# A style-conditioned convolution stack in front of a mixture of experts: layer 0 on four-position blocks with two terms for three, and layer 1's input in planes put together by 4 copies for 16

## The chip, the cores and the metric

The kernel runs on one core of a Trainium2 chip. The metric is the device time of one execution in microseconds; less is better. TensorE (PE) does the matmuls, VectorE (DVE), ScalarE (ACT) and GpSimd (POOL) the elementwise work, and SyncE (SP) issues most DMAs. Each engine runs its own instruction stream in program order and waits on semaphores.

## What is computed

The input is 128 samples of 32 channels and 512 positions. Four convolution layers with kernels that depend on the sample's style (`same`, `upsample`, `same`, `downsample`) turn x into hidden states of the same shape. Each of the 128 x 32 = 4096 rows of 512 is then a token for a layer of 16 experts with top-4 routing and one shared expert; the sum is added to x. Cut to what matters:

```python
def _layer(x, style, w, b, mw, mb, typ):
    s = style @ mw.T + mb                       # one factor for each sample and input channel
    weight = SCALE * w * s[:, None, :, None]
    demod = lax.rsqrt(jnp.sum(weight * weight, axis=(2, 3)) + EPS)
    weight = weight * demod[:, :, None, None]
    # 'same': 3-tap convolution; 'upsample': transposed convolution, then blur;
    # 'downsample': blur, then 3-tap convolution of stride 2
...
scores = sigmoid(x @ gate_w.T) + bias
topk_w, topk_idx = jax.lax.top_k(scores, 4)
...
out = sum over the experts of cw * (silu(x @ Wg.T) * (x @ Wu.T)) @ Wd.T
out = out + silu(x @ Sg.T) * (x @ Su.T) @ Sd.T
return x_input + out
```

## The kernel before

Every product is made at nearly full float32 precision from float32r halves: each operand is split into a high part and a low part (the rest), and a product is three matmuls, high x high, high x low and low x high. `hi_passes` (L202) issues the two that need only the high part of the data, `lo_passes` (L209) the third, which also needs the low part. So a convolution of n terms (n matrices against n shifted views of the data) is 3n matmuls.

**Groups.** The convolution stage works through G = 32 groups of 4 samples x 32 channels = 128 partitions. `body(g)` is written for each engine, and the engines' bodies are one software pipeline: in body g PE does layer 0 of group g + 1, layers 1, 2 and 3 of group g, and for group g - 1 the transposes, the shared expert's products and the router's logits. Its order is: layer 0, prefix of the masks, transposes, layer 1, up products, layer 2, turning z, logits, down products, layer 3. The order is written out by hand, and only semaphores tie the engines together. Most bodies run in a loop of two bodies a turn.

**Layout.** In layers 1 to 3 a matrix of 128x128 holds the taps for four positions at once: partitions are 4 positions (Q = 4) x 32 channels, and the free dimension is sample and block. Layer 0 is different: partitions are 4 samples x 32 channels, a matrix is block diagonal over the samples, and the three taps are three matrices against x0 shifted by 0, 1 and 2 positions. As each partition has its own sample and channel, its style factor is one scalar (`own`, filled by `owns` in the start), applied by ACT in `first_in` (L497, x0_hi) and by DVE in `first_in` (L716, x0_lo), both reading `xraw`.

**From layer 0 to layer 1.** ACT evacuates bank 0 into t1 with one instruction (L511), even and odd positions apart. DVE splits t1 into x1p (high L766, low L760). SP's `stack` (L300) then copies x1p to x1, in which the partitions are 4 shifted positions x 32 channels: 16 copies from SBUF to SBUF, one for each of 4 position planes and 4 samples, of 32 partitions x 2 x 255 or 256 elements. Layer 1 on PE waits for `x1_stacked`, and so does DVE before it writes x1p again.

**The chain on DVE.** DVE's body g does the placement of group g - 2 (L777 to L786), xt_lo (L790), x1p of group g + 1, x2 of group g in two halves (L800, L802, L760), the gated product z (L808, L809), x3 of group g in two halves (L826, L831, L760), the router's top-4 for group g - 1 (L839 to L859), then x0_lo of group g + 2 (L716) and the output row (L867). PE's low passes of layer 0 wait for x0_lo.

**GpSimd** fills constants in the start, waits for `fill_written` (three DMAs of SP behind its loads), issues two DMAs, and in the stage issues four indirect DMAs a group, the `scatter` of the group's list entries, when DVE's placement is ready. **SP** issues, in each body: the stack of group g + 1, the load of xraw for group g + 3, the output and the next xbase, and four writes of h_rows.

After the stage follow the tables of the expert jobs and the expert stage (from about 600 us), which the change doesn't touch.

## Time and profile before

| | |
|---|---|
| median of 3 runs | 1265.27 us (1263.3 to 1267.74) |
| the profiled execution | 1267.31 us, its span 1265.6 us |
| PE, DVE, ACT, GpSimd busy | 91%, 68%, 38%, 43% of the span |
| start, 0 to 60 us | PE busy 31.85 us |
| groups, 60 to 560 us | PE busy 465.04 us, DVE 402.86 us, ACT 248.40 us, GpSimd 126.03 us |
| between the stages, 560 to 600 us | PE busy 14.38 us |
| experts, from 600 us | PE busy 645.70 us |
| mean granted TensorE clock | 0.97 of full speed |

The profile is of one execution, on its one core. Busy times count instructions that run; an idle time stands in brackets ahead of the instruction that ends it, with the instruction that released it. A matmul's length includes its filling; the distance from one start to the next says how fast they follow each other.

### The profile page before, as it was taken

The numbers are of one execution on the slowest core, as the hardware profiler recorded it, in microseconds if no ns is written. First come the engines' busy times: TensorE is split into PE (matmuls) and PEld (weight loads), VectorE is DVE, ScalarE is ACT, GpSimd is POOL, SyncE is SP. The second block draws the span as 40 slices with busy tenths as digits, with TensorE's granted clock in tenths as the row PEclk, the third lists the DMA queues.
The fourth block names the chain that finished last, engine by engine and source line by source line (L and its number), as shares of the span: only waits on it lengthen the run. The fifth ranks groups of instructions, "written<-read, shape, count | busy, mean of one in ns | idle before, by whom it ended". The sixth has DMA issues, their size and how long they took to land. (4 is left out here: it accounts for less than half of the span.)

```text
span 1265.6 us, 25736 instructions
## 1 busy us (share of the span) xinstructions
PE 1157.0 (91%) x7065; PEld 996.7 (79%) x7066; DVE 857.2 (68%) x2456; ACT 483.0 (38%) x1087; POOL 545.5 (43%) x634
## 2 busy tenths in 40 slices
PE   4699999999999999982999999999999999999995
PEld 3476777777777777761998999999998988999995
DVE  8387788878887878875556565655656665555653
ACT  4354445545544454431333232332324332232321
POOL 0012222222222222232565656666666565666663
PEclk9699999999999999995999999999999999999998
DMA  4356444444444444432666766576666767666664
GB/s 153 89 132 179 121 126 129 126 128 129 129 127 128 129 128 131 119 82 92 147 120 151 127 152 120 112 160 120 152 119 159 193 113 162 116 115 116 109 113 77
DMA packets 115059, 162.24 MB, mean 128 GB/s; under 512 B 22880, under 2 KB 72096, under 8 KB 113504
## 3 DMA queue, kind: packets, MB, share of 16 engines
q0 software_dynamic: 35616, 74.08, 32.0%
q1 hardware_dynamic: 78128, 87.93, 24.6%
q10 hardware_dynamic: 1296, 0.01, 0.1%
q8 instruction: 7, 0.11, 0.0%
q14 instruction: 12, 0.10, 0.0%
HBM read 73.28 MB, written 55.18 MB: 102 GB/s over the span
## 5 line engine op out<-in xcount | busy, mean ns | idle before, releaser
L388 POOL DMA_INDIRECT lists<-entry,place x128 | 134.2, 1048 | 431.2 <-DVE place L786 400.0
L1178 PE MATMUL bank<-xt_hi,wup_hi 128*128 128x256 f32 x1104 | 271.8, 281 | 1.9 <-ACT xt_hi L594 1.6
L1178 PE MATMUL bank<-xt_hi,wup_lo 128*128 128x256 f32 x1104 | 271.9, 280 | 0.0
L419 POOL DMA_INDIRECT out_rows<-yb,sid x140 | 228.1, 1629 | 89.8 <-DVE yb L959 64.8
L1178 PEld LDWEIGHTS bank<-xt_hi,wup_hi 128*128 128x128 f32 x1104 | 208.9, 189 | 6.8 <-ACT xt_hi L594 2.0
L1178 PEld LDWEIGHTS bank<-xt_hi,wup_lo 128*128 128x128 f32 x1104 | 207.9, 188 | 2.8
L406 POOL DMA_INDIRECT xg<-h_rows,gid x140 | 141.4, 1010 | 112.7 <-PE bank L1156 65.8
L1182 PE MATMUL bank<-xt_lo,wup_hi 128*128 128x256 f32 x1104 | 173.8, 280 | 0.0
L959 DVE TENSOR_SCALAR yb<-bank,all_lists 128x512 f32<-128x512 f32 x138 | 100.3, 748 | 90.8 <-DMA out_rows<-yb,sid 57.0
L202 PE MATMUL bank<-x_hi,cwt_hi 128*128 128x512 f32 (+1 forms) x352 | 139.8, 400 | 13.9 <-DVE x_hi L831 10.5
L502 ACT ACTIVATE t<-bank,cB,cA 128x256 f32<-128x256 f32 x256 | 127.3, 569 | 59.8 <-PE bank L209 50.4
L1182 PEld LDWEIGHTS bank<-xt_lo,wup_hi 128*128 128x128 f32 x1104 | 148.8, 188 | 0.0
L611 ACT ACTIVATE zt_hi<-z 128x256 fp32r<-128x256 f32 x138 | 57.6, 418 | 229.1 <-DVE z L949 219.1
L202 PE MATMUL bank<-x_hi,cwt_lo 128*128 128x512 f32 (+1 forms) x352 | 138.0, 392 | 0.0
L607 ACT ACTIVATE sg<-bank 128x256 f32<-128x256 f32 x138 | 52.7, 382 | 209.7 <-PE bank L1182 184.6
L209 PE MATMUL bank<-x_lo,cwt_hi 128*128 128x512 f32 (+1 forms) x352 | 105.2, 400 | 21.5 <-DVE x_lo L716 21.5
L1194 PE MATMUL bank<-wdn_hi,zt_hi 128*128 128x512 f32 x276 | 115.1, 417 | 2.4 <-ACT zt_hi L611 2.4
L1196 PE MATMUL bank<-wdn_hi,zt_lo 128*128 128x512 f32 x276 | 109.2, 396 | 0.0
L1194 PE MATMUL bank<-wdn_lo,zt_hi 128*128 128x512 f32 x276 | 108.9, 395 | 0.0
L202 PEld LDWEIGHTS bank<-x_hi,cwt_hi 128*128 128x128 f32 x352 | 67.9, 193 | 42.0 <-issue 23.7
L209 PEld LDWEIGHTS bank<-x_lo,cwt_hi 128*128 128x128 f32 x352 | 63.3, 194 | 47.8 <-DVE x_lo L716 34.9
L760 DVE TENSOR_TENSOR zt_lo<-z,zt_hi 128x256 fp32r<-128x256 f32 x138 | 58.8, 426 | 61.9 <-ACT zt_hi L611 54.7
(208 smaller groups left out, 2105.7 us busy)
## 6 DMA issues: line engine op xcount, KB each, us to landing
x<-x1p SPq DMA_DIRECT2D x256, 64.0 KB
x<-x1p SPq DMA_DIRECT2D x256, 63.8 KB
wraw<-in_Wup SPq DMA_DIRECT2D x11, 1024.0 KB
xraw<-in_x SPq DMA_DIRECT2D x32, 256.0 KB, 2.6
xbase<-in_x SPq DMA_DIRECT2D x32, 256.0 KB
h_rows<-hrow SPq DMA_DIRECT2D x128, 64.0 KB
out_rows<-orow SPq DMA_DIRECT2D x32, 256.0 KB, 2.0
wdraw<-in_Wdn SPq DMA_DIRECT2D x11, 512.0 KB
```

What stands on the lines that cost most here:

```text
L202: r = pe.matmul(dst, lhs[a if data_moves else 0], rhs[0 if data_moves else a], start=n == 0 and a == 0, stop=False)
L209: r = pe.matmul(dst, lhs[0 if data_moves else 1], rhs[1 if data_moves else 0], start=False, stop=last and n == len(terms) - 1)
L388: pool.indirect_dma_start(out=lists, out_offset=bass.IndirectOffsetOnAxis(ap=place[:, par, k:k + 1], axis=0), in_=entry[:, par, k, :], in_ ...
L406: pool.indirect_dma_start(out=xg[:, u, :], out_offset=None, in_=h_rows, in_offset=bass.IndirectOffsetOnAxis(ap=gid[:, u:u + 1], axis=0)).t ...
L419: pool.indirect_dma_start(out=out, out_offset=bass.IndirectOffsetOnAxis(ap=sid[:, u:u + 1], axis=0), in_=yb[:, u, :], in_offset=None, comp ...
L502: r = act.activation(dst[:, n], src[:, n], ACT.Identity, scale=cA[:, l, bass.ds(g * NB + b, 1)], bias=cB[:, l, bass.ds(g * NB + b, 1)])
L760: return dve.tensor_tensor(lo, src, hi.bitcast(F32), ALU.subtract)
L959: dve.tensor_scalar(yb[:, u, :], bank[6 + u][:], all_lists[:, bass.ds(at + u, 1), 1], None, ALU.mult).then_inc(S["b_y"], 1)
L1178: pe.matmul(dst, lhs[a], rhs[0], start=k == 0 and a == 0, stop=False)
L1182: r = pe.matmul(dst, lhs[0], rhs[1], start=False, stop=k == HC - 1)
L1194: pe.matmul(bank[6 + u][:], zt[0][:, u, c, :], wdn[b][a][:, c, :], start=c == 0 and a == 0, stop=False)
L1196: r = pe.matmul(bank[6 + u][:], zt[1][:, u, c, :], wdn[b][0][:, c, :], start=False, stop=c == IC - 1)
```

## The change

The host lays x out a second time, as `xq`: partitions are 4 positions x 32 channels, with 4 samples x 130 blocks, one position of padding ahead of the row (and zeros behind). Layer 0 then has the layout of the later layers: each matrix holds the taps for four positions, and two matrices (this block and the next) take the place of three. Its output has 4 positions in the partitions and 4 samples x 128 blocks in the free dimension.

- One partition now carries all four samples, so that the style factor is no longer a scalar of the partition. `own` and `owns` fall away. GpSimd multiplies `xraw` in place by `s` (`scaled`, new), ACT only copies to x0_hi and waits for GpSimd (`xs_ready`), DVE subtracts to get x0_lo. Four `scaled` stand ahead of GpSimd's loop, the others in it, each ahead of the scatter of four groups before.
- ACT's evacuation of layer 0 is four instructions by `evac`, one for each sample, where it was one.
- x1p is 4 positions x 32 channels by now, so x1 is made from it by 4 copies of 96 or 32 partitions. x1, t2, x2 and t3 keep even and odd blocks in two planes of 128. In layer 2 the second matrix needs the next block, which lies in the other plane; its matmuls are made for each plane, 256 columns each.
- xraw, x0_hi and x0_lo have 520 columns, where they had 512, 514 and 514.

The core of the diff (the changed memsets, shapes and waits of the same kind are left out):

```diff
-    UP, SAME, DOWN, SQ = K, K + 1, K + 3, K + 6
+    FIRST, UP, SAME, DOWN, SQ = 0, 2, 3, 5, 8
...
+    V = L // Q
+    VP = xq.shape[3]
+    STACKS = 4
...
-        xraw = sb("xraw", [P, 2, L])
+        xraw = sb("xraw", [P, 2, NB, VP])
-        x0 = [sb("x0_hi", [P, L + 2], F32R), sb("x0_lo", [P, L + 2], F32R)]
-        x1p = sb("x1p", [P, 2, 2, L // 2], F32R)
-        x1 = sb("x1", [P, 2, NB, W], F32R)
-        x2 = [sb("x2_hi", [P, NB, W + 2], F32R), sb("x2_lo", [P, NB, W + 2], F32R)]
+        x0 = [sb("x0_hi", [P, NB, VP], F32R), sb("x0_lo", [P, NB, VP], F32R)]
+        x1p = sb("x1p", [P, 2, NB, V], F32R)
+        x1 = sb("x1", [P, 2, NB, 2, V], F32R)
+        x2 = [sb("x2_hi", [P, NB, 2, V + 2], F32R), sb("x2_lo", [P, NB, 2, V + 2], F32R)]
...
 # SP, stack(g)
-                for q, (plane, src, dst) in enumerate(((1, 0, 1), (0, 0, 0), (1, 0, 0), (0, 1, 0))):
-                    n = W - src - dst
-                    for b in range(NB):
-                        sp.dma_start(x1[C * q:C * q + C, :, b, dst:dst + n].bitcast(F32),
-                                     x1p[C * b:C * b + C, :, plane, src:src + n].bitcast(F32)).then_inc(S["x1_stacked"], 16)
+                for plane, to, part, rows, back in ((0, 1, 0, 3, 0), (0, 0, 3, 1, 1), (1, 0, 1, 3, 0), (1, 3, 0, 1, -1)):
+                    dst = slice(max(back, 0), V + min(back, 0))
+                    src = slice(max(-back, 0), V + min(-back, 0))
+                    sp.dma_start(x1[C * to:C * (to + rows), :, :, plane, dst].rearrange("p a b u -> p (a b) u").bitcast(F32),
+                                 x1p[C * part:C * (part + rows), :, :, src].rearrange("p a b u -> p (a b) u").bitcast(F32)).then_inc(S["x1_stacked"], 16)
...
 # GpSimd
-            with pool.Fori(0, G // 2) as it:
+            def scaled(g, par, k):
+                pool.wait_ge(S[f"x_loaded{par}"], 16 * (k + 1))
+                land(pool)
+                pool.tensor_tensor(xraw[:, par], xraw[:, par], s[:, 0, bass.ds(g * NB, NB)].rearrange("p (b a) -> p b a", a=1).broadcast_to([P, NB, VP]),
+                                   ALU.mult).then_inc(S["xs_ready"], 1)
+
+            pool.wait_ge(S["s_ready"], 1)
+            for g in range(4):
+                scaled(g, g % 2, g // 2)
+            with pool.Fori(0, (G - 4) // 2) as it:
                 for u in range(2):
+                    scaled(it * 2 + (u + 4), u, it + 2)
                     scatter(it * 2 + u, u)
+            for g in range(G - 4, G):
+                scatter(g, g % 2)
...
 # ACT, first_in and layer0
-                act.wait_ge(S[f"x_loaded{par}"], 16 * (k + 1))
+                act.wait_ge(S["xs_ready"], g + 1)
                 land(act)
-                act.activation(x0[0][:, 1:L + 1], xraw[:, par, :], ACT.Copy, scale=own[:, 0, bass.ds(g, 1)]).then_inc(S["x0_hi"], 1)
+                act.activation(x0[0][:], xraw[:, par], ACT.Copy).then_inc(S["x0_hi"], 1)
...
-                act.activation(t1[:], bank[0][:].rearrange("p (w two) -> p two w", two=2), ACT.Identity,
-                               scale=own[:, 1, bass.ds(g, 1)], bias=own[:, 2, bass.ds(g, 1)]).then_inc(S["t1_ready"], 1)
+                evac(g, range(NB), bank[0][:].rearrange("p (b v) -> p b v", b=NB), t1, 0, S["t1_ready"])
...
 # DVE, first_in
-                dve.scalar_tensor_tensor(out=x0[1][:, 1:L + 1], in0=xraw[:, par, :], scalar=own[:, 0, bass.ds(g, 1)],
-                                         in1=x0[0][:, 1:L + 1].bitcast(F32), op0=ALU.mult, op1=ALU.subtract).then_inc(S["x0_lo"], 1)
+                minus(x0[1][:], xraw[:, par], x0[0][:]).then_inc(S["x0_lo"], 1)
...
 # PE, layer0
-                same = [([w[:, k, :] for w in cwt], [x[:, k:k + L] for x in x0], True) for k in range(K)]
+                dst = bank[0][:].rearrange("p (b v) -> p b v", b=NB)
+                same = [columns(FIRST + m, P, lambda a: x0[a][:, :, m:m + V]) for m in range(2)]
...
 # PE, layer 2
-                        terms = [columns(SAME, P, lambda a: x2[a][:, both, 0:W]),
-                                 columns(SAME + 1, P, lambda a: x2[a][:, both, 1:W + 1])]
+                        here = [columns(SAME, P, lambda a: x2[a][:, both, :, 0:V])]
+                        following = [[columns(SAME + 1, P, lambda a: x2[a][:, both, 1 - r, r:r + V])] for r in range(2)]
...
-                        hi_passes(pe, dst, terms)
+                        hi_passes(pe, dst, here)
+                        for r in range(2):
+                            for a in range(2):
+                                pe.matmul(dst[:, :, r], cwt[a][:, SAME + 1, :], following[r][0][1][0], start=False, stop=False)
...
-                        lo_passes(pe, dst, terms).then_inc(S["l2_done"], 1)
+                        lo_passes(pe, dst, here, last=False)
+                        for r in range(2):
+                            ins = lo_passes(pe, dst[:, :, r], following[r], last=r == 1)
+                        ins.then_inc(S["l2_done"], 1)
```

How the instructions stand on GpSimd, from the two DMAs of the start to the loop of the stage. Before, with `lists<-entry,place` the scatter and L392 the loop:

```order
L382 DMA out_rows<-zrow 128x512 x2
L392 UNCONDITIONAL_BRANCH
L392 ISA
L388 DMA lists<-entry,place 65536x2 x4
L385 REGISTER_ALU
L388 DMA lists<-entry,place 65536x2 x4
L392 REGISTER_ALU
L392 COMPARE_AND_BRANCH
```

Now, with `xraw<-xraw,s` the new product:

```order
L386 DMA out_rows<-zrow 128x512 x2
L399 TENSOR_TENSOR xraw<-xraw,s 128x520 x4
L405 UNCONDITIONAL_BRANCH
L405 ISA
L399 ISA
L399 TENSOR_TENSOR xraw<-xraw,s 128x520
L389 REGISTER_ALU
L392 DMA lists<-entry,place 65536x2 x4
L399 ISA
L399 TENSOR_TENSOR xraw<-xraw,s 128x520
L389 REGISTER_ALU
L392 DMA lists<-entry,place 65536x2 x4
```

Each scatter of the loop has a product ahead of it, and four products stand between the start's DMAs and the loop.

On PE, layer 0 in body 2, ahead of the prefix of the masks (`bank<-mask,tri`). Before:

```order
L202 MATMUL bank<-x_hi,cwt_hi 128x512
L202 MATMUL bank<-x_hi,cwt_lo 128x512
L202 MATMUL bank<-x_hi,cwt_hi 128x512
L202 MATMUL bank<-x_hi,cwt_lo 128x512
L202 MATMUL bank<-x_hi,cwt_hi 128x512
L202 MATMUL bank<-x_hi,cwt_lo 128x512
L209 MATMUL bank<-x_lo,cwt_hi 128x512 x3
L1043 MATMUL bank<-mask,tri 128x16
```

Now:

```order
L206 MATMUL bank<-x_hi,cwt_hi 128x512
L206 MATMUL bank<-x_hi,cwt_lo 128x512
L206 MATMUL bank<-x_hi,cwt_hi 128x512
L206 MATMUL bank<-x_hi,cwt_lo 128x512
L213 MATMUL bank<-x_lo,cwt_hi 128x512 x2
L1048 MATMUL bank<-mask,tri 128x16
```

Two high passes and one low pass are gone.

On SP, the first stack, with the load of xraw behind it; `h_rows<-zrow` and `lists<-all_lists` are the fills that GpSimd waits for. Before:

```order
L290 DMA h_rows<-zrow 128x512 x2
L291 DMA lists<-all_lists 128x1024
L300 DMA x<-x1p 32x2x255 x4
L300 DMA x<-x1p 32x2x256 x8
L300 DMA x<-x1p 32x2x255 x4
L306 DMA xraw<-in_x 128x512
```

Now:

```order
L293 DMA h_rows<-zrow 128x512 x2
L294 DMA lists<-all_lists 128x1024
L304 DMA x<-x1p 96x8x128
L304 DMA x<-x1p 32x8x127
L304 DMA x<-x1p 96x8x128
L304 DMA x<-x1p 32x8x127
L310 DMA xraw<-in_xq 128x520
```

Sixteen copies of 32 partitions have become two of 96 and two of 32, and the load of xraw stands twelve copies nearer.

## Rows read from the trace of the kernel before

**Rows 1.** The stretch of the 32 groups: busy time (and instructions) of each engine.
```profile
60.00:560.00 500.00, 465.04 (x2223) 359.13 (x2221) 402.86 (x1488) 248.40 (x549) 126.03 (x120) 1.00 0.49 128
```

**Rows 2.** Page, part 2: granted clock of TensorE, 40 slices of 31.6 us.
```profile
PEclk9699999999999999995999999999999999999998
```

**Rows 3.** Waits from 60 to 560 us: total us, times, longest.
```profile
PE bank L209 <- DVE x_lo L716: 20.4, 29, 1.0
```

**Rows 4.** Timeline of PE: the first and the last of those 29 waits.
```profile
72.47 0.96 PE L209 MATMUL bank<-x_lo,cwt_hi 128*128 128x512 f32 x3 [0.52 <-DVE x_lo L716]
...
533.84 0.97 PE L209 MATMUL bank<-x_lo,cwt_hi 128*128 128x512 f32 x3 [0.52 <-DVE x_lo L716]
```

**Rows 5.** Timeline of PE in one group: start, length, idle before.
```profile
303.13 0.97 PE L209 MATMUL bank<-x_lo,cwt_hi 128*128 128x512 f32 x3 [0.78 <-DVE x_lo L716]
...
307.74 1.09 PE L209 MATMUL bank<-wup_hi,xt_lo 128*128 128x512 f32 x4
...
315.44 0.48 PE L202 MATMUL bank<-x_hi,cwt_hi 128*128 128x512 f32 x1 [0.58 <-DVE x_hi L831]
```

**Rows 6.** Timeline of ACT in the same group.
```profile
305.17 0.78 ACT L511 ACTIVATE t<-bank,own 128x512 f32<-128x512 f32 x1
...
311.39 1.02 ACT L502 ACTIVATE t<-bank,cB,cA 128x256 f32<-128x256 f32 x2 [2.14 <-PE bank L209]
...
318.15 1.50 ACT L502 ACTIVATE hrow<-bank,cB,cA 128x128 f32<-128x128 f32 x4 [1.28 <-PE bank L209]
```

**Rows 7.** Timeline of DVE in the same group.
```profile
312.47 0.06 DVE L826 MEMSET t<- 64x2 f32 x1 [1.40 <-issue]
...
313.03 0.69 DVE L760 TENSOR_TENSOR x_lo<-t,x_hi 128x512 fp32r<-128x512 f32 x1
...
319.09 0.75 DVE L716 SCALAR_TENSOR_TENSOR x_lo<-xraw,own,x_hi 128x512 fp32r<-128x512 f32 x1
```

**Rows 8.** GpSimd in the same group: the last of the four scatter issues.
```profile
310.71 0.97 POOL L388 DMA_INDIRECT lists<-entry,place  x1 [0.30 <-issue]
```

**Rows 9.** Timeline of PE in the expert stage.
```profile
800.24 0.28 PE L1178 MATMUL bank<-xt_hi,wup_hi 128*128 128x256 f32 x1
800.36 0.28 PE L1178 MATMUL bank<-xt_hi,wup_lo 128*128 128x256 f32 x1
```

**Rows 10.** SP's queue in the same group.
```profile
307.48 10.20 SPq L300 DMA_DIRECT2D x<-x1p  x16
```

**Rows 11.** Packets of one queue, 28 to 40 us, then 57 to 60.5 us.
```profile
q1 hardware_dynamic: 1296, 1.08, 38.2%
...
q1 hardware_dynamic: 576, 0.26, 29.6%
```

**Rows 12.** Timeline of the start, all engines.
```profile
16.00 0.71 ACT L497 ACTIVATE x_hi<-xraw,own 128x512 fp32r<-128x512 f32 x1
...
18.60 1.38 POOL L382 DMA_DIRECT2D out_rows<-zrow  x2 [16.09 <-DMA lists<-all_lists]
...
19.70 1.75 DVE L723 RECIPROCAL d<-dv 128x256 f32<-128x256 f32 x1 [0.64 <-ACT dv L568]
...
22.02 0.76 DVE L671 COPY own<-cA 32x32 f32<-32x32 f32 x4
...
26.95 0.42 DVE L766 CAST x1p<-t 128x512 fp32r<-128x512 f32 x1
...
28.13 10.35 SPq L300 DMA_DIRECT2D x<-x1p  x16
...
40.08 0.77 PE L202 MATMUL bank<-x,cwt_hi 128*128 128x512 f32 x1 [9.61 <-DMA x<-x1p]
```

**Rows 13.** GpSimd operations that read, and DVE beside the second.
```profile
1.96 0.29 POOL L373 TENSOR_SCALAR_AFFINE_SELECT ident<-ident 128x128 f32<-128x128 f32 x1 [0.16 <-POOL ones L371]
...
958.95 0.72 POOL L429 COPY sid<-sid_next 128x2 int32<-128x2 int32 x1
958.96 1.28 DVE L749 TENSOR_TENSOR wup_lo<-wraw,wup_hi 128x512 fp32r<-128x512 f32 x2
```

More of the change, by code:

```diff
@@ L248, in matrices @@
                 rows = slice(C * q, C * q + C)
-                copy(big[rows, 0:K, q, :], mats[rows, 0:K])
                 copy(big[rows, SQ:SQ + 4, q, :], mats[rows, NT:NT + 4])
@@ L665, in _ @@
             dve.memset(tsum[:], 0.0).then_inc(S["consts_done"], 1)
-            def owns(n, a):
-                for b in range(NB):
-                    rows = slice(C * b, C * b + C)
-                    r = dve.tensor_copy(own[rows, n, :], a[rows, 0, :].rearrange("p (g b) -> p g b", b=NB)[:, :, b])
-                return r
             dve.wait_ge(S["taps_loaded"], 16 * Q)
@@ L1014, in turn_z, with columns @@
                 return r
+            def columns(m, rows, data):
+                return [w[0:rows, m, :] for w in cwt], [data(a) for a in range(2)], True
             def layer0(g):
@@ L1020, in layer0 @@
                     pe.wait_ge(S["t1_ready"], g)
[L1021 removed]
+                dst = bank[0][:].rearrange("p (b v) -> p b v", b=NB)
+                same = [columns(FIRST + m, P, lambda a: x0[a][:, :, m:m + V]) for m in range(2)]
                 pe.wait_ge(S["x0_hi"], g + 1)
[L1023 removed]
+                hi_passes(pe, dst, same)
                 pe.wait_ge(S["x0_lo"], g + 1)
[L1025 to L1029 removed]
+                lo_passes(pe, dst, same).then_inc(S["l0_done"], 1)
             def body(g, par, tail=0):
```

67 lines of the change are left out of this document (33 added, 34 removed).

## Prediction

> **What bounds the kernel now.** I read the stages first. Between 60 and 560 us, where the 32 groups run, PE is busy 465 of 500 us at full granted clock, DVE 403, ACT 248, GpSimd 126 [rows 1, 2]. So the change touches a stage in which PE nearly always works, and the first thought is that each matmul removed is time won. The waits correct this: PE stands 29 times, 0.70 us on average, in front of the same instruction, the first low pass of layer 0, until DVE has written x0_lo [rows 3]. The first and the last of these waits end at 72.47 and 533.84 us [rows 4], so 28 groups take 16.48 us each.
>
> In one group at 303 us, PE starts the low passes of layer 0 at 303.13 after a wait of 0.78; the other wait of note is for DVE's x3_hi at 315.44, 0.58 [rows 5]. The loop closes through three engines: PE (from the layer-0 low passes to the first half of layer 2) -> ACT (evacuates that half at 311.39 [rows 6]) -> DVE (starts on it at 312.47 and works almost without a gap through x3, the logits and the top-4 to x0_lo at 319.09 [rows 7]) -> PE. What PE does between layer 2 and the layer-0 high passes is not on this loop. So the group is timed by PE's first half and DVE's second half, and a saving or a delay counts only if it lies on that loop.
>
> **Layer 0, nine matmuls to six.** A full 512-column matmul follows the last one after (1.09 - 0.40)/3 = 0.23 us [rows 5]. Four of the six passes that are kept stand ahead of the x0_lo wait, as six of nine did: the two removed there only lengthen the wait. One low pass is removed behind it: -0.23 us a group on the loop. x0_lo itself becomes a plain subtraction: 0.75 [rows 7] to what L760 takes for 512 columns, 0.69, and 1.6% for 520: -0.05. Sum -0.28; 28 groups: -8 us. If PE alone set the pace, it would be 3 x 0.23 x 28 = -19 us; that is the far bound on the good side.
>
> **Layer 2, split into halves.** Per group, six 512-column matmuls become twelve of 256 columns. In the expert stage 256-column matmuls, each with its own weight load, follow each other at 0.12 us [rows 9], half of 0.23: nothing gained or lost.
>
> **ACT's evacuation of layer 0** goes from one instruction of 0.78 to four of 128 columns. Four such take 1.50 us for hrow [rows 6]: +0.72 us. ACT is busy half of the stage [rows 1], but behind this instruction it evacuates layer 1, and DVE waits for both: x1p and then x2 come later. What hides it is that DVE reaches t1 only after its eight placement operations, and that PE has the expert's up products between layer 1 and layer 2. I cost it at nothing; with that cover gone it is at most 0.72 a group, 20 us.
>
> **The stack of x1, 16 copies to 4.** SP issues 16 in 10.2 us [rows 10]. The bytes stay; packets go from 1024 or 1020 bytes to 512 or 508, so there are 2048 for 1024. A packet of the present stack takes 0.382 x 16 x 12 us / 1040 = 70 ns, counting the sixteen semaphore writes of each copy as free; a 512-byte packet of h_rows 0.296 x 16 x 3.5 / 512 = 32 ns [rows 11]. The new stack therefore occupies the 16 engines for 4.1 us at 32 ns up to 9.0 us at 70 ns. I take 5.5. In the loop that hides: the issue ends at 317.7 [rows 10], and PE takes the stack in layer 1 of the next group, behind the layer-0 wait, at about 321; the new one is through earlier. Only the first stack, at 28 us, is waited for: 9.61 us of PE [rows 12].
>
> **GpSimd multiplies xraw by the style.** This is new: 32 products of 128x520 with two SBUF inputs, in place, one for each group, put ahead of each group's scatter. The trace has no such operation. From below: no faster than DVE's 0.69 for a product-like operation of 512 columns [rows 7]. From above: an affine_select reads and writes 128 columns in 0.29 us [rows 13]; four times that is 1.18, and doubled for the second input 2.4. I take 1.2, since the 0.29 holds a fixed part. GpSimd has the time (126 us of 500), and ACT needs the result a group later.
>
> The question is DVE. A GpSimd copy of two elements took 0.72 us, against 0.29 for 128 columns, when it began at 958.95 beside DVE's subtraction of two SBUF tensors at 958.96, and ended when the first of the two was over [rows 13]. So the two engines exclude each other there. The reverse, DVE behind a long GpSimd read, no row shows: its price lies between 0 and the whole operation. The Trainium skill (SBUF — State Buffer, "Who interferes with whom") says that whoever issues first holds the shared pair for the whole instruction and the other "fully blocks". It thus speaks against this change: by that rule DVE loses most of the product's length in each group, case (c) below; of it this trace shows the one order, DVE first and GpSimd waiting, and the other not. The Trainium skill (GPSIMD Engine Reference, "Elementwise — side-by-side cycle accounting") has 4497 ns for 2048 columns of such a sum, by which an estimate for 520 is 1.14 us, and the term below would be +26 us.
>
> Where does it fall? SP starts the stack at about 307.5 and has issued its four copies after 2.6 us at today's 0.65 each [rows 10]; xraw follows and queues behind the stack's data. With 1.6 us of latency (40.08 less the end of issue, 38.48 [rows 12]) and 4.1 to 9.0 us of data it lands between 313 and 318 us of this group. GpSimd's scatter is over at 311.7 [rows 8]. So the product starts inside DVE's run from 312.47 to 319.84, which is on the loop, and not in the idle 1.40 us before it [rows 7]. Almost all of DVE there is of the excluded kind: casts and subtractions from SBUF, then small operations that wait for each other. If DVE waits for the product, it loses about 1.0 of the 1.2 us (some reads of PSUM go on). I take 1.0 us for 27 groups: +27 us. What is behind DVE's waiting instruction is x3, then the whole top-4 chain and x0_lo; PE would wait longer at both places.
>
> **The start.** Today ACT makes x0_hi at 16.00. GpSimd, which must now come first, stands until 18.60 for the fill of the lists and then issues two DMAs for 1.38 us [rows 12]; 1.2 of product follow: 21.2. ACT's x0_hi ends at 21.9 instead of 16.7. Behind it on ACT stand the table load and the square root: DVE's reciprocal, now at 19.70, starts about 23.9, +4.2. DVE's copies into own fall away (0.76 for cA, the like for cB): -1.5. So x1p moves from 26.95 by +2.7. From the first stack issue at 28.13 to PE at 40.08 were 11.95 us [rows 12]; with 5.5 us of data, and 2.5 for the first packet's and the last landing's latency, about 8: -4. Start together: -1.3, between -3 (data 4.1) and +2.5 (data 9.0). One further group with layer 0 at the end of its chain gives -0.7.
>
> **Sum.** -8 - 1.3 - 0.7 + 27 = +17 us on the profiled execution's 1267.3 (span 1265.6 and 1.7 around it), which is 2.0 above the median of the runs: 1265.3 + 17 = 1282 us.
>
> **Rivals.**
>
> (a) GpSimd's product costs DVE nothing: it waits or reads between DVE's operations, as the short copy did without delaying the next DVE instruction. Then -10: 1255 us, faster. For it speaks that DVE's pair in [rows 13] took 1.28 us, twice 0.69 less the usual overlap: the copy did not hold up the second. The sign turns at a delay of 10/27 = 0.37 us a group. Chance 0.34.
>
> (b) It costs a part, 0.25 to 0.5 us a group, since it begins late in DVE's run or gets in only at a gap: 1262 to 1269 us. Chance 0.12.
>
> (c) My forecast, 0.6 to 1.2 us a group: 1271 to 1288. Chance 0.42.
>
> (d) The waits grow so long that the granted clock falls. It fell only in the slices of the start and of the end of the stage, 0.6 and 0.5 on the page [rows 2], where PE idled for microseconds. A twentieth of the stage at half clock would add 25 us: 1300 or more. Chance 0.07.
>
> (e) Issue of the large copies grows with their packets: 10.2 us for 1024 packets would be 20 us for 2048, more than a group of 16.5. SP would then set the pace, +4 us a group, 1390 us. All 16 copies today are issued at the same cadence with data hardly filling the engines (38%), so I give it 0.05.
>
> **How the numbers follow.** What a measurement of this kernel tells from no change is about 0.3%, 4 us. Faster: (a), less where the ACT term eats into it, and nothing of the rest: 0.35. Within: most of (b): 0.10. Slower: (c), (d), (e) and the rest of (b): 0.55. The range must take in (a) and (c) and leaves out the ends of (d) and (e) and the best of (a): 1251 to 1292. Case (c) alone would be 1271 to 1288.
>
> **What would show it.** In the profile after: 256-column matmuls of layer 2 at 0.12 us; a layer-0 wait of about 0.70 + 0.47 us on x0_lo; the product's length, and where it lies; DVE's subtractions of 0.69 and its casts that are stretched or late beside it, and a group above 17 us where (c) holds, 16.2 where (a) does; PE's first layer-1 matmul at about 39 us. I am wrong if DVE's durations stay what they were with the product beside them, or if the copy lands late.

## The result and the profile after

The changed kernel takes 1293.82 us (median of 4 runs, 1288.15 to 1298.19), the kernel before 1264.7 us in its runs (1263.3 to 1267.74): ratio 1.0225, 95% interval 1.0199 to 1.025. The forecast was 1282 us in a range of 1251 to 1292.

The page and the stretch from 60 to 560 us of the changed kernel (busy time, PE's row of tenths, granted clock; then one row of the windows view, its columns as in [rows 1]):

```profile
PE 1157.5 (89%) x7160; PEld 996.7 (77%) x7161; DVE 868.6 (67%) x2444; ACT 499.3 (39%) x1185; POOL 581.6 (45%) x666
...
PE   3798888888889898894699999999999999999995
...
PEclk9799999999999999997799999999999999999998
```
```profile
60.00:560.00 500.00, 436.03 (x2187) 333.76 (x2186) 394.49 (x1409) 247.39 (x602) 151.19 (x140) 0.99 0.45 123
```

PE's tenths fall from 9 to 8 in most slices of the loop, while its granted clock stays as in [rows 2]: PE waits more, it doesn't run slower. Its waits in the same stretch (total us, times, longest), beside the 20.4 us of [rows 3]:

```profile
PE bank L213 <- DVE x_lo L721: 32.2, 27, 1.5
PE bank L206 <- DVE x_hi L835: 20.3, 26, 1.5
PE bank L206 <- ACT zt_hi L558: 7.4, 10, 1.0
```

The timeline of the changed kernel, from the start to the last group used below (start, duration, in brackets the idle time before and what ended it):

```profile
21.15 2.10 POOL L399 TENSOR_TENSOR xraw<-xraw,s 128x520 f32<-128x520 f32 x2
...
31.77 2.87 SPq L304 DMA_DIRECT2D x<-x1p  x4
38.31 0.77 PE L206 MATMUL bank<-x,cwt_hi 128*128 128x512 f32 x1 [4.67 <-DMA x<-x1p]
71.27 0.19 PE L1048 MATMUL bank<-mask,tri 128*128 128x16 bf16 x1
268.13 0.39 ACT L554 ACTIVATE sg<-bank 128x256 f32<-128x256 f32 x1
269.42 0.17 PE L206 MATMUL bank<-x_hi,cwt_hi 128*128 128x4 f32 x1
271.88 1.02 ACT L518 ACTIVATE t<-bank,cB,cA 128x256 f32<-128x256 f32 x2 [3.36 <-PE bank L213]
272.95 0.06 DVE L830 MEMSET t<- 64x2 f32 x1 [2.19 <-ACT t L518]
312.06 1.05 POOL L399 TENSOR_TENSOR xraw<-xraw,s 128x520 f32<-128x520 f32 x1 [3.74 <-DMA xraw<-in_xq]
312.13 1.00 DVE L721 TENSOR_TENSOR x_lo<-t3f,x_hi 64x4 fp32r<-64x4 f32 x1
329.45 0.70 DVE L721 TENSOR_TENSOR x_lo<-t,x_hi 128x512 fp32r<-128x512 f32 x1
329.49 1.57 POOL L399 TENSOR_TENSOR xraw<-xraw,s 128x520 f32<-128x520 f32 x1 [3.78 <-DMA xraw<-in_xq]
330.85 0.24 DVE L846 TENSOR_TENSOR sc<-sig,biasrow 128x16 f32<-128x16 f32 x1 [0.28 <-ACT sig L570]
559.68 0.19 PE L1048 MATMUL bank<-mask,tri 128*128 128x16 bf16 x1
```

The reader is to see four things.
- **Start.** The first two products take GpSimd 2.10 us from 21.15 on. The four copies are issued in 2.87 us for the 10.35 of [rows 12], and layer 1 begins at 38.31 for 40.08.
- **Loop.** The matmul of mask and tri stands once in each group. From its first to its 29th there are 488.41 us, 17.44 us a group; before it is 461.37 and 16.48. The whole stage, from the first to the 32nd of them, takes 531.3 us for 503.6: this is the loss.
- **The product and DVE keep each other out.** At 312.13 a DVE operation on 64x4 elements takes 1.00 us and ends with GpSimd's product of 1.05; the same operation takes 0.17 where GpSimd is idle. In the next group DVE's subtraction of 0.70 at 329.45 was there first and GpSimd takes 1.57. In 18 of the first 28 groups an operation of DVE is 0.5 to 0.9 us longer for it; these groups take 18.1 us on average, the others 16.2. Over the 28 groups DVE's operations beside the product are 13.8 us longer in all, 0.49 a group.
- **Layer 2's evacuation starts late.** The first half of layer 2 ends on PE where the 128x4 matmul of the second half starts (269.42). ScalarE, idle since 268.52, starts to evacuate it only at 271.88, and DVE waits 2.19 us for that. I call the distance from that 128x4 matmul to the evacuation the **lag**. Over the 28 groups it has a mean of 1.61 us and is mostly near 0.4, 1.0, 1.7 or 2.5. Before, its mean is 0.72 and its highest value 1.35. The prediction doesn't speak of it. The trace's semaphore records, which no view prints, tell more: the signal by which PE says that the first half is done comes at 271.64, 2.22 us behind the start of the 128x4 matmul, and ScalarE's wait ends 0.02 us later. The signal is recorded in 25 of the 32 groups, and in all of these the wait ends within 0.03 us of it. Where the lag is 0.4 us (after_2 below) the signal comes 0.18 us behind the 128x4 matmul. So ScalarE isn't slow to answer: PE's completion of the half, or its signal, is late. The ends of matmuls are modelled in the profile, so that the trace can't say which of the two.

The expert stage, which the change doesn't touch, adds its own: from the first transpose of gathered rows to the end 676.1 us for 670.8.

### The profile page after: what moved, and what is told of

The parts are those of the page before. It is cut to its first block and busy times, and to the rows that moved or that the text cites. A ratio compares the mean times of both kernels' runs of the same rounds, so it can differ in the third digit from the quotient of the medians.

```text
span 1296.5 us, 25739 instructions
## 1 busy us (share of the span) xinstructions
PE 1157.5 (89%) x7160; PEld 996.7 (77%) x7161; DVE 868.6 (67%) x2444; ACT 499.3 (39%) x1185; POOL 581.6 (45%) x666
## 3 DMA queue, kind: packets, MB, share of 16 engines
q0 software_dynamic: 35616, 74.08, 32.2%
## 5 line engine op out<-in xcount | busy, mean ns | idle before, releaser
L1190 PE MATMUL bank<-xt_hi,wup_hi 128*128 128x256 f32 x1104 | 275.3, 282 | 1.8 <-ACT xt_hi L609 1.5
L1190 PE MATMUL bank<-xt_hi,wup_lo 128*128 128x256 f32 x1104 | 274.8, 282 | 0.0
L392 POOL DMA_INDIRECT lists<-entry,place x128 | 133.9, 1046 | 266.6 <-DVE place L789 235.4
L518 ACT ACTIVATE t<-bank,cB,cA 128x256 f32<-128x256 f32 (+1 forms) x384 | 172.1, 541 | 86.8 <-PE bank L213 65.8
L206 PE MATMUL bank<-x_hi,cwt_hi 128*128 128x512 f32 (+1 forms) x256 | 105.9, 417 | 32.1 <-DVE x_hi L835 22.9
L213 PE MATMUL bank<-x_lo,cwt_hi 128*128 128x512 f32 (+2 forms) x384 | 99.9, 368 | 33.0 <-DVE x_lo L721 33.0
L399 POOL TENSOR_TENSOR xraw<-xraw,s 128x520 f32<-128x520 f32 x32 | 38.0, 1189 | 151.5 <-DMA xraw<-in_xq 151.5
L206 PE MATMUL bank<-x_hi,cwt_lo 128*128 128x512 f32 (+1 forms) x256 | 100.9, 394 | 0.0
```

Of the source, the lines that this page charges most:

```text
L206: r = pe.matmul(dst, lhs[a if data_moves else 0], rhs[0 if data_moves else a], start=n == 0 and a == 0, stop=False)
L213: r = pe.matmul(dst, lhs[0 if data_moves else 1], rhs[1 if data_moves else 0], start=False, stop=last and n == len(terms) - 1)
L392: pool.indirect_dma_start(out=lists, out_offset=bass.IndirectOffsetOnAxis(ap=place[:, par, k:k + 1], axis=0), in_=entry[:, par, k, :], in_ ...
L518: r = act.activation(dst[:, n], src[:, n], ACT.Identity, scale=cA[:, l, bass.ds(g * NB + b, 1)], bias=cB[:, l, bass.ds(g * NB + b, 1)])
L1190: pe.matmul(dst, lhs[a], rhs[0], start=k == 0 and a == 0, stop=False)
```

## The experiments

Behind the first measurement the runs fall into five groups, each on one chip and each with the kernel before timed beside it. That showed two kinds of chip: **slow chips**, where it takes 1265 to 1268 us (the first measurement was on one), and **fast chips**, where it takes 1251. There were three measurements on each kind. The five groups were on five different chips (that of the first measurement isn't on record), so it isn't shown that the chip makes the difference, and not, say, something that changed between the groups; "fast chip" stands for "the chips on which the kernel before took 1251 us". So a kernel's loop is compared only with loops on the same kind. Even there it differs: the changed kernel's group is 17.44 us on one slow chip and 17.29 on another, 15.93 and 15.95 on two fast chips; so a difference between two slow chips is good to some 0.15 us. The group and the lag of a row come from one profiled execution each. "Group" is the distance from the first to the 29th matmul of mask and tri, divided by 28; where an edit changes numbers, tokens go to other experts and the expert stage changes its length (a_noprod adds 142 blocks of rows to the output, the kernel before 140), so only the group is compared there, and the ratio beside "output differs" says little.

| kernel | chip | first, 29th, us | group, us | mean lag, us | ratio to before (95%) |
|---|---|---|---|---|---|
| before | slow | 73.27, 534.64 | 16.48 | 0.72 | 1 |
| changed | slow | 71.27, 559.68 | 17.44 | 1.61 | 1.0225 (1.0199–1.025) |
| after_4 (changed) | slow | 70.89, 555.12 | 17.29 | 1.36 | 1.0215 (1.018–1.0251) |
| b_two | slow | 72.54, 526.02 | 16.20 | 0.59 | 0.9937 (0.9913–0.9962), output differs |
| b_evac4 | slow | 72.33, 543.91 | 16.84 | 1.03 | 1.0088 (1.0054–1.0121) |
| a_onevac_2 | slow | 70.29, 527.46 | 16.33 | 0.77 | 0.9981 (0.9956–1.0005), output differs |
| a_noprod_onevac | slow | 67.69, 516.66 | 16.03 | 0.83 | 1.0148 (1.0109–1.0187), output differs |
| a_split4_unroll | slow | 71.53, 542.00 | 16.80 | 1.19 | 1.014 (1.0111–1.017) |
| before_2 (before) | fast | 73.26, 519.66 | 15.94 | 0.41 | 1 |
| after_2, after_3 (changed) | fast | 71.46, 517.52 and 70.31, 516.80 | 15.93, 15.95 | 0.41 | 1.0023 (1.0006–1.0041), 1.0011 (0.9992–1.0029) |
| a_noprod | fast | 68.48, 507.38 | 15.67 | 0.41 | 1.0048 (1.0034–1.0062), output differs |
| a_onevac | fast | 69.73, 510.18 | 15.73 | 0.41 | 0.9991 (0.9975–1.0008), output differs |
| a_unroll, a_unroll_2 | fast | 69.93, 518.49 and 70.93, 516.34 | 16.02, 15.91 | 0.31 | 1.0009 (0.9991–1.0028), 1.0018 (1.0–1.0037) |
| a_stack16 | fast | 73.30, 520.12 | 15.96 | 0.41 | 1.0065 (1.0045–1.0085) |
| b_product | fast | 76.86, 531.63 | 16.24 | 0.41 | 1.0103 (1.0071–1.0134) |
| b_unroll | fast | 71.74, 516.95 | 15.90 | 0.32 | 1.0001 (0.9981–1.0021) |
| a_scale4 | fast | 66.81, 524.35 | 16.34 | 0.45 | 1.0096 (1.0062–1.013) |
| a_split4 | fast | 68.85, 511.41 | 15.81 | 0.41 | 0.999 (0.9972–1.0008) |

**a_noprod** leaves the product out.

```diff
-                pool.tensor_tensor(xraw[:, par], xraw[:, par], s[...], ALU.mult).then_inc(S["xs_ready"], 1)
+                pool.sem_inc(S["xs_ready"], 1)
```


> The changed kernel with the product of x and s left out (GpSimd only passes the semaphore on, so layer 0 reads x without s). If the collision of GpSimd's product with DVE carries the loss, the loop falls from 531.3 us to about 496 (503.6 less 8) and the time to about 1257 us. If ScalarE's late start of layer 2's evacuation carries it (1.5 us behind its matmuls on average after, 0.75 before), that lag stays and only the stretched DVE operations go, 0.7 to 0.9 us in about 17 groups: about 1280 us.

**a_onevac** puts one activation in the place of the four that evacuate layer 0.

```diff
-                evac(g, range(NB), bank[0][:].rearrange("p (b v) -> p b v", b=NB), t1, 0, S["t1_ready"])
+                act.activation(t1[:]..., bank[0][:], ACT.Identity, scale=cA[:, 0, bass.ds(g * NB, 1)],
+                               bias=cB[:, 0, bass.ds(g * NB, 1)]).then_inc(S["t1_ready"], 1)
```


> The changed kernel with layer 0's result evacuated by one activation of 128x512 with one sample's scale, in place of four of 128x128 (the numbers of three samples in four are scaled wrongly). If ScalarE's four evacuations make it late, ScalarE gains 0.6 to 0.8 us a group, the lag in layer 2 falls back to 0.4 to 1.3 us and the time to 1265 to 1275 us. If the product alone carries the loss: 1288 to 1294 us.

**a_unroll** writes ScalarE's loop out (b_unroll is the same in the kernel before).

```diff
-            with act.Fori(0, (G - 6) // 2) as it:
-                body(it * 2 + 3, 1, (it + 1, it + 2))
-                body(it * 2 + 4, 0, (it + 2, it + 2))
+            for g in range(3, G - 3):
+                body(g, g % 2, (g // 2, (g + 1) // 2))
```


> The changed kernel with ScalarE's loop over groups 3 to 28 written out, so that its scales' places are constants and no register is worked out ahead of an activation; nothing else differs. If ScalarE's lag comes from its instruction stream (register instructions and waits on registers), it falls to 0.3 us as in the written-out group at 71.3 us and the time to about 1270 us or less. If it comes from DMA traffic or the product, nothing changes: 1288 to 1298 us.

**a_stack16** splits each of the four stack copies by sample.

```diff
-    STACKS = 4
+    STACKS = 16
...
+                    for b in range(NB):
+                        sp.dma_start(x1[C * to:C * (to + rows), :, b, plane, dst]..., x1p[C * part:C * (part + rows), :, b, src]...)
```


> The changed kernel with each of the four stack copies split by sample, 16 copies again. If the bulk of four copies in 2.8 us delays ScalarE, its lag falls back to 0.4 to 1.3 us and the time by some 15 us, to about 1278; x_raw also lands some 7 us later, so the product falls elsewhere in the group. If the four copies have no part in it: the issue of 10 us stays hidden and the time is 1288 to 1298 us, unless the later product hits another DVE operation.

All four ran on one fast chip and were within 1% of the kernel before, where 1.02 was the base of every expectation. a_noprod's 1257.78 us is the time expected of a collision that carries the loss, but its loop stage took 480.2 us where 496 was expected. The group was short in a_noprod (15.67 us) and in a_onevac (15.73), and in a_stack16 and a_unroll, which keep product and evacuations, as well (15.96, 16.02). The long lags were gone in all four. No one edit can have done that, and the changed kernel itself hadn't run on that chip, so both kernels ran again.

**before_2 and after_2**, unchanged.

> The kernel before once more, on the chip of the runs beside it. If the chip matters, ScalarE's lag in layer 2 is a steady 0.4 us here as in the last four runs, a group takes under 16.3 us and the time is 1250 to 1255 us. If those runs owed it to their edits, the lag is 0.4 to 1.3 us as in the trace of before, a group 16.48 us.

> The changed kernel once more. If its lag of 1.0 to 2.6 us is the change's own, it is here too and the ratio to before is about 1.02 (1.020 to 1.025 measured first). If it belongs to the chip of the first run, the lag is 0.4 us, groups take about 15.9 us and the ratio is about 1.00.

Timelines of before_2, then of after_2:

```profile
73.26 0.18 PE L1043 MATMUL bank<-mask,tri 128*128 128x16 bf16 x1
519.66 0.18 PE L1043 MATMUL bank<-mask,tri 128*128 128x16 bf16 x1
1139.06 0.38 PE L1156 MATMUL bank<-ident,xg 128*128 128x128 f32 x2
1176.15 0.38 PE L1156 MATMUL bank<-ident,xg 128*128 128x128 f32 x2
```
```profile
71.46 0.18 PE L1048 MATMUL bank<-mask,tri 128*128 128x16 bf16 x1
253.19 0.17 PE L206 MATMUL bank<-x_hi,cwt_hi 128*128 128x4 f32 x1
253.61 1.02 ACT L518 ACTIVATE t<-bank,cB,cA 128x256 f32<-128x256 f32 x2 [1.33 <-PE bank L213]
258.67 1.05 POOL L399 TENSOR_TENSOR xraw<-xraw,s 128x520 f32<-128x520 f32 x1 [4.08 <-DMA xraw<-in_xq]
259.13 0.62 DVE L846 TENSOR_TENSOR sc<-sig,biasrow 128x16 f32<-128x16 f32 x1 [0.28 <-ACT sig L570]
517.52 0.19 PE L1048 MATMUL bank<-mask,tri 128*128 128x16 bf16 x1
1133.95 0.27 PE L1168 MATMUL bank<-ident,xg 128*128 128x128 f32 x1
1171.41 0.27 PE L1168 MATMUL bank<-ident,xg 128*128 128x128 f32 x1
```

Here ScalarE's evacuation follows 0.41 to 0.42 us behind the 128x4 matmul in every looped group of both kernels, and the loop is worth nothing either way (15.94 and 15.93). The product now meets the tail of DVE's operation on `sc` (0.62 us, 0.17 alone; on average 0.24 us over in the looped groups). So the loss of 27.7 us in the loop is not the change's on every chip: it appears on the slow chips. On a fast chip the parts can be read one by one. The product costs 15.93 − 15.67 = 0.26 us a group, the four evacuations 15.93 − 15.73 = 0.20, and the rest of the change gives 15.94 − (15.73 − 0.26) = 0.47 back. Sixteen copies for four change nothing in the loop (15.96), but the first group comes at 73.30 for 71.46.

**b_product** adds to the kernel before only the product, in place on `xraw` with the factors of `own`.

```diff
+                pool.tensor_tensor(xraw[:, par, :], xraw[:, par, :], own[:, 0, bass.ds(g, 1)].broadcast_to([P, L]), ALU.mult)...
...
-                act.activation(x0[0][:, 1:L + 1], xraw[:, par, :], ACT.Copy, scale=own[:, 0, bass.ds(g, 1)])
+                act.activation(x0[0][:, 1:L + 1], xraw[:, par, :], ACT.Copy)
```


> The kernel before with one thing of the change: the product of x and s on GpSimd in place in x_raw (128x512), ScalarE's copy and DVE's subtraction without a scale. If the product's collision with DVE costs 0.7 to 0.9 us in a group, 1.015 of before; if it falls where DVE has nothing due, 1.000.

> The kernel before with ScalarE's loop over groups 3 to 28 written out. If register work and waits on registers hold ScalarE up by 0.4 us a group on average (lag 0.72 to 0.31), 0.990 of before on a chip where the lag is 0.72; if the lag is a steady 0.4, 0.996 to 1.000.

The product costs 0.30 us a group here and 3.6 us at the start: 76.86 for 73.26. In the changed kernel it is 3.0 us at the start (71.46 for a_noprod's 68.48). b_unroll takes 0.1 us off the lag and nothing measurable off the time: where the signal comes in time, ScalarE's register work costs nothing.

**a_scale4** has no product; ScalarE and DVE scale by sample. **a_split4** cuts the product into four instructions. after_3 is the changed kernel.

```diff
a_scale4
-                act.activation(x0[0][:], xraw[:, par], ACT.Copy).then_inc(S["x0_hi"], 1)
+                for b in range(NB):
+                    r = act.activation(x0[0][:, b], xraw[:, par, b], ACT.Copy, scale=s[:, 0, bass.ds(g * NB + b, 1)])
...
+                    r = dve.scalar_tensor_tensor(out=x0[1][:, b], in0=xraw[:, par, b], scalar=s[:, 0, bass.ds(g * NB + b, 1)],
+                                                 in1=x0[0][:, b].bitcast(F32), op0=ALU.mult, op1=ALU.subtract)
a_split4
+                for b in range(NB):
+                    r = pool.tensor_tensor(xraw[:, par, b], xraw[:, par, b], s[:, 0, bass.ds(g * NB + b, 1)].broadcast_to([P, VP]), ALU.mult)
```


> The changed kernel a third time, to see which kind of chip this call has: with ScalarE's lag a steady 0.4 us, groups of 15.9 us and a ratio of 1.00, as in after_2, or with a lag of 1.0 to 2.6 us, groups of 17.4 us and 1.02, as in the first measurement. It is the base for the runs beside it.

> The changed kernel without the product: ScalarE writes x0_hi by four activations with the sample's scale, DVE x0_lo by four scalar_tensor_tensor, GpSimd only scatters. If the product costs 0.26 us a group and 3 us at the start, and the longer ScalarE and DVE work is hidden, the time is 10 us under the changed kernel (0.994 of before). If four short instructions for one cost their 0.7 us on ScalarE and 0.3 us on DVE as the evacuation's did (0.20 us a group in all), 1.000 to 1.003.

> The changed kernel with GpSimd's product in four instructions of 128x130. If one GpSimd instruction keeps DVE out until it ends, DVE waits at most for a quarter, 0.3 us, and its excess on the instruction that meets the product falls from a mean of 0.24 us to 0.1 or less: 2 to 4 us less than the changed kernel. If four starts on GpSimd lengthen the whole, DVE meets more pieces and the time is the same or up to 5 us more.

> The changed kernel with ScalarE's loop written out, once more. On a chip where the changed kernel's lag is 0.4 us: 0.31 us, and within 0.3% of the changed kernel, as in a_unroll. On a chip where it is 1.0 to 2.6 us: if ScalarE's looping instruction stream is what makes it late, 0.3 us here too, and 1.5 to 2% less than the changed kernel; if not, no difference.

Two rows of a_scale4's timeline, and one of a_split4's:

```profile
203.20 1.31 ACT L508 ACTIVATE x_hi<-xraw,s 128x130 fp32r<-128x130 f32 x4
...
213.23 1.15 DVE L722 SCALAR_TENSOR_TENSOR x_lo<-xraw,s,x_hi 128x130 fp32r<-128x130 f32 x4
```
```profile
207.73 1.48 POOL L400 TENSOR_TENSOR xraw<-xraw,s 128x130 f32<-128x130 f32 x4 [3.98 <-DMA xraw<-in_xq]
```

Without the product and with one instruction each, the group took 15.67 us; with four short ones for one on both engines, 16.34. That is 0.67 us a group, more than twice the product that it saves. Four pieces of product take GpSimd 1.48 us for 1.05, and yet the group is 0.14 us shorter than after_3's, as expected if DVE waits for a piece and not for the whole. With 1243.0 us its profiled span is the shortest of all, but its ratio of 0.999 can't be told from 1. a_unroll_2 repeats a_unroll: nothing gained.

**A slow chip** came next. after_4 is the changed kernel, a_split4_unroll has the product in four instructions and ScalarE's loop written out. b_two leaves the third tap out of layer 0's sum in the kernel before; b_evac4 evacuates layer 0 there with four instructions.

```diff
b_two
-                same = [([w[:, k, :] for w in cwt], [x[:, k:k + L] for x in x0], True) for k in range(K)]
+                same = [... for k in range(2)]
b_evac4
+                for n in range(4):
+                    r = act.activation(t1[:, :, 64 * n:64 * n + 64], bank[0][:, 128 * n:128 * n + 128]..., ACT.Identity, ...)
```


> The changed kernel a fourth time, as the base of this call: lag 0.4 us, 15.9 us a group and a ratio of 1.000 to 1.003, or, on a chip like that of the first measurement, a lag of 1.0 to 2.6 us and 1.02.

> The changed kernel with the product in four instructions and ScalarE's loop written out: the version that the runs so far point to. If both gains hold, 15.75 us a group and a ratio of 0.998; on a chip with the lag of the first measurement it tells whether a written-out stream ends the lag: then 0.31 us and a ratio of 0.98 to 0.99, else 1.01 or more.

> The kernel before with layer 0 in two terms for three (taps 0 and 1; the third is left out of the sum), nothing else. If only one low pass of layer 0 lies on the loop, as the prediction has it: 0.25 to 0.30 us a group less than the kernel before, 15.65 on a chip with 15.94. If all three passes do: 0.7 us less, 15.25. If the loop is DVE's at that place: nothing. The output differs, and with it which experts the tokens go to, so the loop is compared and not the end.

> The kernel before with layer 0's result evacuated by four activations of 128x128 in place of one of 128x512, with the same scale. If the four lie on the loop, as the difference between the changed kernel and a_onevac says, 0.20 us a group more (16.14 on a chip with 15.94), a ratio of 1.004; if they are covered, as the prediction has it, no difference.

A group of a_split4_unroll, then one of b_evac4 and its first and 29th groups:

```profile
243.41 0.17 PE L206 MATMUL bank<-x_hi,cwt_hi 128*128 128x4 f32 x1
245.76 1.02 ACT L519 ACTIVATE t<-bank,cB,cA 128x256 f32<-128x256 f32 x2 [3.32 <-PE bank L213]
```
```profile
72.33 0.18 PE L1045 MATMUL bank<-mask,tri 128*128 128x16 bf16 x1
...
227.85 0.41 ACT L541 ACTIVATE sg<-bank 128x256 f32<-128x256 f32 x1
229.13 0.18 PE L202 MATMUL bank<-x_hi,cwt_hi 128*128 128x4 f32 x1
231.57 1.02 ACT L502 ACTIVATE t<-bank,cB,cA 128x256 f32<-128x256 f32 x2 [3.31 <-PE bank L209]
...
543.91 0.18 PE L1045 MATMUL bank<-mask,tri 128*128 128x16 bf16 x1
```

The loss is back with the chip. A written-out stream does not end the lag (2.35 us in the group shown), so the theory that register work on ScalarE makes it falls. b_evac4 shows lags of up to 2.5 us in the old kernel, with no product, no new stack copies and no new layer 0: four evacuations are enough to lengthen it from a mean of 0.72 to 1.03. They cost 0.36 us a group, 0.9% in all. b_two gives 0.28 us a group. Both are set against the 16.48 of another slow chip; b_evac4's ratio, measured beside the kernel before on its own chip, agrees (11 us, of which 28 groups at 0.36 are 10). On the same chip as after_4, a_split4_unroll's group is 0.49 us shorter, with a mean lag of 1.19 for 1.36: on a slow chip the product in one piece costs more than the 0.14 us of a fast one.

**The last two**, on a slow chip again, undo the evacuations with and without the product (edits as above).

> The changed kernel with layer 0 evacuated in one activation, product kept. On a chip with before at 1251 us: 15.7 us a group, as in a_onevac. On a chip with before at 1265 us: if the evacuations carry most of the loss there, the lag is back at 0.4 to 0.8 us and the ratio at 1.000 to 1.005; if the product does, 1.01 or more.

> The changed kernel without the product of x and s and with layer 0 evacuated in one activation with one sample's scale. If the two costs add up on a chip with before at 1251 us: 15.94 less 0.26 less 0.20, about 15.5 us a group; if they overlap, 15.65. On a chip with before at 1265 us: a lag of at most 0.72 us and about 15.9 us a group. The output differs, so the loop is compared.

```profile
70.29 0.19 PE L1049 MATMUL bank<-mask,tri 128*128 128x16 bf16 x1
294.49 1.05 POOL L399 TENSOR_TENSOR xraw<-xraw,s 128x520 f32<-128x520 f32 x1 [3.49 <-DMA xraw<-in_xq]
294.54 1.55 DVE L722 TENSOR_TENSOR x_lo<-t,x_hi 128x512 fp32r<-128x512 f32 x1
359.44 0.69 DVE L722 TENSOR_TENSOR x_lo<-t,x_hi 128x512 fp32r<-128x512 f32 x1
359.56 1.48 POOL L399 TENSOR_TENSOR xraw<-xraw,s 128x520 f32<-128x520 f32 x1 [3.67 <-DMA xraw<-in_xq]
527.46 0.19 PE L1049 MATMUL bank<-mask,tri 128*128 128x16 bf16 x1
```

These are rows of a_onevac_2. On a slow chip one activation for four takes the changed kernel from 17.29 or 17.44 to 16.33 us a group, below the 16.48 of before. That is 0.96 to 1.11 us for 28 groups, 27 to 31 us, about all that was lost. The product then costs 16.33 − 16.03 = 0.30, much as on a fast chip. The rows show how: of the groups with a lag near 1.0 us, eight have the product begin just ahead of DVE's subtraction, which grows from 0.69 to 1.55 us, and take 16.9 to 17.0 us; in five the subtraction is first, GpSimd waits, and they take 16.1 to 16.2. So a collision in which DVE loses costs about its length, as the prediction has it; it happens in some groups only.

One run is missing: the changed kernel without the product but with its four evacuations, on a slow chip. So the 0.96 to 1.11 us is what the evacuations cost beside the product. In the old kernel, without it, they cost 0.36. The 0.60 to 0.75 us between, 17 to 21 us in 28 groups, is there only with both, and taking the product away might have undone it too.

## Why the prediction was wrong

On the first chip the sign was right and the time was 12 us short of the measured one; the reason given for the loss was one part of it. The sign was luck in so far as the chip decided it: on fast chips the same change makes no difference of note (1.0023 and 1.0011). Between the two profiled executions lie +31 us where the sum has +17: −2.0 before the first group, +27.7 in the loop stage, for which the sum has −8 and +27, and +5.3 in the expert stage, for which it has nothing. Point by point:

- **Layer 0, one low pass on the loop, −0.28 us a group: right.** b_two, which has the fewer passes and not the plain subtraction, measures 0.28, its slightly lower mean lag included, for the 0.23 of the pass. PE's waits for x0_lo grew from 0.70 to 1.19 us on average (32.2 us in 27 waits), in after_2 to 1.17 (33.9 in 29); 1.17 was forecast. The whole of the change without product and evacuations gives 0.45 to 0.47 back; the 0.17 to 0.19 above the third term come from parts that I costed at nothing and didn't try apart.
- **ScalarE's evacuation, +0.72 us, costed at nothing: this is the step that failed.** The prediction named 20 us as its price if the cover is gone, and took no case for it. It costs 0.20 us a group (5.6 us) on a fast chip; on a slow one 0.36 us without the product (b_evac4) and 0.96 to 1.11 us a group, 27 to 31 us, beside it (a_onevac_2). There it lengthens the lag behind layer 2. The trace of before had that lag already (0.31 to 1.35 us), and I read none of it: I asked whether ScalarE was busy, and it was idle for long stretches; I didn't ask how late the signal that it waited for came.
- **GpSimd's product, 1.0 us of DVE for 27 groups: the mechanism was right, the size not.** DVE and GpSimd do exclude each other, and the product takes 1.05 us where 1.2 was estimated. But on a fast chip it meets the tail of one short operation. Undone, it gives 0.26 to 0.30 us a group, 7 to 8 us for 27. The 0.5 to 0.9 us in 18 groups of the first measurement, 13.8 us in all, came with the lag: with few exceptions (two in after_4), the product falls on a long piece of layer 2's part only where DVE starts late on it. In a_split4_unroll, groups with a lag of 1.6 us take 17.2 us; in the changed kernel, with the product in one piece and a lag of 1.7 us, 17.75. So DVE's own loss beside the product is half of the sum's 27 us, and that only on the slow chips; what else the loop lost goes with the lag, which the sum doesn't have. How much of that lag needs the product too is open, as said above.
- **Start, −1.3 us: nearly right, by two errors that cancel.** It was −1.8 for layer 1 and −2.0 for the first group. x1p came 3.65 us later (30.60), not 2.7, as GpSimd's wait for the fill ended at 19.79 and not at 18.60; from the first stack issue at 31.77 to PE were 6.5 us, not 8. a_stack16 gives the gain back (73.30), so it is the four copies'. The product, 1.2 us in the prediction's chain, costs 1.7 us by layer 1 (38.06 in after_2, 36.40 in a_noprod) and 3.0 by the first group.
- **Four stack copies and split layer 2, nothing: right for the copies** (15.96 against 15.93 and 15.95 a group), not tried apart for layer 2, whose 256-column matmuls do follow each other at 0.12 us (268.45, 268.57, 268.69, 268.81).
- **Expert stage, not in the sum: +5.3 us.** It takes 670.8 us before and 676.1 after; on fast chips 670.0 and 676.2. Four jobs take 37.09 us in before_2 and 37.46 in after_2, with the granted clock at full speed in both. All runs of the old kernel and its variants have 669.6 to 671.9 us; those of the new one 672.3 to 676.7, a_noprod and a_noprod_onevac left out, where more rows are added. So a second term is missing from the sum, and why it is there is open: tiles lie at other addresses, and nothing here tests that.
- **The rivals.** (d) and (e) didn't come: the granted clock stayed at [rows 2]'s level, and four large copies are issued in 2.87 us. (b), 0.25 to 0.5 us a group, is where the product is on a fast chip (0.26 and, in b_product, 0.30), and on a slow one behind a single evacuation (0.30); (a), it costs nothing, didn't come; no rival has the lag. The signs named for (c), a group above 17 us and stretched operations of DVE, came on the slow chips, and were not enough to tell (c) from the lag. Summed with what was measured, the slow chip has −2.0 at the start, +27.7 in the loop stage and +5.3 in the expert stage, the 31 us between the spans of 1265.6 and 1296.5. The fast one has −1.8, −0.3 in 28 groups, +1.2 behind them and +6.2 in the expert stage: 1249.0 to 1254.3.

**Open.** What makes the signal late on slow chips was not found. In every profile from a slow chip it is PE's signal for layer 2 that comes late, and that for the turned z, by 0.2 to 0.5 us in most groups; PE's signals for layers 0, 1 and 3 come 0.01 us behind the matmul's modelled end, as all of PE's do on fast chips. In the changed kernel, groups with a lag of 1.0 and of 2.5 us have the same times just before it, within about 0.1 us in the looped groups, for the sigmoid, the stack copies' issue and the scatters. Product (b_evac4 has none), register work (a_split4_unroll) and the new copies (b_evac4 has the old ones) are each excluded as its only cause. That without the four evacuations the loss is gone is shown by a_onevac_2; that they alone make it is not, as the product stands beside them. And no version beat the kernel before by more than can be measured: a_split4's 0.999 on a fast chip and a_onevac_2's 0.9981 (0.9956 to 1.0005) on a slow one, the latter with one sample's scale for four, are the best.

## What to carry to other kernels

Four short instructions for one long one on an engine that looks idle are not free: where another engine waits for the last of them, they lay 0.2 us a group on the loop on one kind of chip, and on the other 0.36 by themselves and about 1.0 beside the product. Look in the trace how long after the instruction that an engine waits for it starts, not only whether it is busy, and look at the signal between the two before you call the waiting engine slow. An instruction of GpSimd that keeps DVE out costs not its length but what it meets, here 0.26 us a group, and in four pieces half as much. Two terms that are tried away one at a time can each seem to be the whole loss; the run without the one and with the other has to be made for both. And before a loss of 2% is put down to a change, both kernels should run on a second chip: here the same pair gave 1.0225 and 1.0215 on two, 1.0023 and 1.0011 on two others.

## What the runs showed of the hardware

- **Two kinds of chip.** The same program takes 1265 to 1268 us on some and 1251 on others. The difference is not in the instructions' durations (their medians agree within 0.01 us) and not in TensorE's clock (0.97 over the span in both profiles of the kernel before), but in when ScalarE can start layer 2's evacuation: on fast chips 0.41 to 0.42 us behind the 128x4 matmul in every looped group of both kernels, on slow chips 0.3 to 1.35 us in the kernel before and up to 2.66 in the changed one. ScalarE's wait ends 0.02 to 0.03 us behind PE's signal in all of them, wherever the signal is recorded; the signal is what comes late. Whether the chip itself makes the difference is not shown: the five groups of runs were on five chips.
- **DVE and GpSimd.** A 64x4 operation of DVE went from 0.17 to 1.00 us beside a product of 128x520; the Trainium skill (SBUF — State Buffer, "Who interferes with whom") has the two sharing ports, so that the one that issues first keeps the other out. The rows agree: DVE's operation at 312.13 ends with the product, and the product at 329.49 takes 1.57 us where DVE's subtraction was first.
- **Short instructions.** Four activations of 128x130 take 1.31 us where one of 128x520 takes 0.69; four of DVE's scalar_tensor_tensor 1.15 where one subtraction of 128x520 takes 0.70; four products on GpSimd 1.48 for 1.05.
